# Prefix sums, slot placing and scatters of a routed graph network: each moved one tile later

## The reference

```python
def _sage_conv(x, edge_index, W_l, W_r, b):
    src, dst = (edge_index[0], edge_index[1])
    agg_sum = segment_sum(x[src], dst, num_segments=x.shape[0])
    agg = agg_sum / maximum(deg, 1.0)[:, None]
    return agg @ W_l + x @ W_r + b
h = relu(_sage_conv(layernorm(x), edge_index, W1_l, W1_r, b1))
x = x + _sage_conv(h, edge_index, W2_l, W2_r, b2)
tokens = layernorm(x)
probs = softmax(tokens @ router_w.T)
rw, re = top_k(probs, 2);  rw = rw / maximum(rw.sum(-1), 1e-12)
combine = zeros((N, 8)).at[arange(N)[:, None], re].set(rw)
out = tokens
for e in range(8):
    y = gelu(tokens @ w1[e] + b1[e]) @ w2[e] + b2[e]
    out = out + combine[:, e:e + 1] * y
return x + out
```

## Time and profile before

| what | us |
|---|---|
| median of 3 timed runs (617.13 to 617.48) | 617.24 |
| the profiled execution | 618.39 |
| span of its records | 616.7 |
| PE busy (90% of the span) | 553.9 |
| DVE busy (60%) | 367.0 |
| POOL busy (29%) | 181.9 |
| third stage, first row of the second aggregation to the first rows loaded for the experts | 293 to 478 |

### The profile page before, as it was taken

The page is one execution under the profiler, slowest core; times in us unless marked ns, Lnnn a source line. Parts: engine busy times, 40 slices in busy tenths (PEclk is TensorE's granted clock), DMA queues, the critical chain, the costliest instruction groups (busy, mean ns, idle before and its releaser), DMA issues.

```text
span 616.7 us, 11244 instructions
## 1 busy us (share of the span) xinstructions
PE 553.9 (90%) x3021; PEld 332.5 (54%) x3022; DVE 367.0 (60%) x1222; ACT 222.8 (36%) x422; POOL 181.9 (29%) x181
## 2 busy tenths in 40 slices
PE   5999989999999999999899999989960799998990
PEld 3544545555555555554354544545430688887880
DVE  5987656766676677662456676765767244443440
ACT  5666835434434444441001000000000355555550
POOL 3740000000000000000211434424355086668884
PEclk9999999999999999999999999999985699999995
DMA  8421211101111110113721347643226367677772
GB/s 267 124 73 60 69 36 52 52 27 52 52 43 36 52 51 28 51 53 56 246 86 53 129 144 242 193 152 129 88 84 230 89 118 129 117 123 115 128 113 30
DMA packets 64343, 61.24 MB, mean 99 GB/s; under 512 B 11281, under 2 KB 62334, under 8 KB 64302
## 3 DMA queue, kind: packets, MB, share of 16 engines
q1 hardware_dynamic: 47422, 44.84, 24.1%
q0 software_dynamic: 11200, 14.40, 12.7%
q10 hardware_dynamic: 5680, 1.49, 1.1%
HBM read 32.34 MB, written 29.30 MB: 100 GB/s over the span
## 4 chain that ended last, share of the span: by engine, by line
PE 61%; DVE 11%; issue 11%; POOL 7%; DMA 6%; ACT 1%; POOLq 1%; DVEq 0%; SPq 0%; ACTq 0%
PE bank L1262 21%; PE counts_ps L635 7%; PE counts_ps L1404 6%; PE bank L1252 6%; PE bank L1177 6%; PE bank L1415 6%; PE counts_ps L1262 4%; POOL xs_dram L570 4%; DMA out<-adj 2%; POOL stat L563 2%; PE counts_ps L1395 2%; POOL out L608 2%; DMA y<-y_dram 1%; PE bank L1167 1%; PE bank L1245 1%
## 5 line engine op out<-in xcount | busy, mean ns | idle before, releaser
L1262 PE MATMUL bank<-y,adj 128*128 128x512 f16 x625 | 154.7, 379 | 0.4 <-ACT zt L1470 0.4
L1262 PE MATMUL counts_ps<-y,adj 128*128 128x512 f16 x625 | 144.5, 379 | 1.9 <-DMA y<-y_dram 1.9
L642 ACT ACTIVATE adj<-counts_ps 128x1000 f32 (+1 forms) x80 | 80.2, 1004 | 61.2 <-PE counts_ps L635 61.2
L608 POOL DMA_INDIRECT out<-adj x56 | 87.0, 1554 | 47.7 <-ACT adj L1603 21.1
L1262 PEld LDWEIGHTS counts_ps<-y,adj 128*128 128x128 f16 x625 | 60.5, 101 | 64.8 <-DMA y<-y_dram 3.9
L1262 PEld LDWEIGHTS bank<-y,adj 128*128 128x128 f16 x625 | 57.8, 97 | 59.5 <-issue 13.7
L546 POOL IOTA onehots<- 128x8 int32 x1 | 0.1, 143 | 231.9 <-PE counts_ps L635 231.9
L1404 PE MATMUL counts_ps<-adj 128*128 128x256 f32 x240 | 58.6, 389 | 2.3 <-ACT adj L1588 2.3
L1567 ACT ACTIVATE rows<-bank 128x256 f32<-128x256 f32 x25 | 9.6, 382 | 128.7 <-PE bank L1336 128.7
L635 PEld LDWEIGHTS counts_ps<-onehots 125*128 125x128 f16 x640 | 41.0, 98 | 27.2 <-issue 10.8
L621 DVE TENSOR_TENSOR onehots<-iota,lo_t 125x1024 f16<-125x1024 f16 x80 | 54.7, 683 | 0.2
(11 more groups left out here) (234 smaller groups left out, 641.0 us busy)
## 6 DMA issues: line engine op xcount, KB each, us to landing
adj<-xs_dram SPq DMA_DIRECT2D x31, 264.0 KB
rows<-z_dram SPq DMA_DIRECT2D x49, 128.0 KB
z_dram<-zt SPq DMA_DIRECT2D x36, 128.0 KB, 1.7
adj<-in_L_ffn_w SPq DMA_DIRECT2D x16, 256.0 KB, 3.2
rows<-in_x SPq DMA_DIRECT2D x24, 128.0 KB
out<-yo SPq DMA_DIRECT2D x24, 128.0 KB
y_dram<-yo SPq DMA_DIRECT2D x23, 128.0 KB, 1.7
y<-y_dram SPq DMA_DIRECT2D x4, 640.0 KB, 6.6
```

The lines of the kernel that those rows point to most:

```text
L608: g.indirect_dma_start(out, bass.IndirectOffsetOnAxis(ap=ids[u][:, h:h + 1], axis=0), ye[u][:, h, :], None, bounds_check=N - 1, oob_is_err ...
L642: nc.scalar.activation(adj[:, :, bass.ds(at, GW * WD)].rearrange("p b (h d) -> p b h d", d=WD), counts_ps[:, 2 * (group % 2):2 * (group % ...
L1262: last = te.matmul(to, adj[:, b, t * P:(t + 1) * P], y[:, b, :], start=(b == 0), stop=(b == NT - 1))
```

## The change

The prefix sums of batches 0 to 4 move from the last block of tiles 5, 9, 13, 17, 21 to block 7 of tiles 6, 10, 14, 18, 22. `place` of these batches moves from the end of the second tile to the third tile, between `x2_and_var` and `norm_and_sum`. A tile is scattered six tiles later and no longer five; after the root of tile 23 two tiles, 17 and 18, are scattered, so that the end is as it was. And the wait for the landing of the scatter before, with its count, is kept only as long as a later tile uses the buffer again, which is up to tile 17.

```diff
-                if t > 0:
+                if 0 < t <= NT - KEPT:
                     pool.wait_ge(scattered[(t - 1) % 2], ((t - 1) // 2 + 1) * (16 * TOPK))
                     pool.sem_inc(S["tok_free"], 1)
...
                 if t == NT - 1:
                     scatter(*to_scatter[t - BATCH - 1])
                 root(t)
-                if BATCH + 1 <= t < NT - 1:
+                if BATCH + 2 <= t < NT - 1:
+                    scatter(*to_scatter[t - BATCH - 2])
+                if t == NT - 2:
                     scatter(*to_scatter[t - BATCH - 1])
...
             for t in range(NT):
                 x2_and_var(t)
+                j = t // BATCH
+                if t % BATCH == 2 and 0 < j < NB - 1:
+                    place(j - 1)
                 if t == NT - 1:
                     place(NB - 2)
                 norm_and_sum(t)
-                j = t // BATCH
                 if t % BATCH == 0 and 0 < j < NB - 1:
                     choose(j - 1)
-                if t % BATCH == 1 and 0 < j < NB - 1:
-                    place(j - 1)
+                if t % BATCH == 2 and 0 < j < NB - 1:
                     if j == MID_BATCH:
...
-                if t % BATCH == 1 and t // BATCH > 0 and t < FIRST_OF[NB - 1]:
-                    between[NT - 1] = [lambda: prefix(t // BATCH - 1)]
+                if t % BATCH == 2 and t // BATCH > 0 and t < FIRST_OF[NB - 1]:
+                    between[7] = [lambda: prefix(t // BATCH - 1)]
```

## The result

The changed kernel takes **611.59 us** (median of 4 runs, 611.18 to 612.18); the kernel before took 617.36 us beside it (4 runs, 617.13 to 618.30). The ratio is 0.990, with an interval from 0.989 to 0.992: 5.8 us are gone, and by the interval between 5.1 and 7.0. Predicted were 6.6 us and 610.6 us. The 6.6 us lie inside that interval too. The profiled execution took 611.19 us, its span is 609.5 us.

What follows compares the result with a forecast made beforehand. PE was taken to set the pace, losing time waiting for DVE's masks. Gains of 6.3 us from its stops and 0.3 from dropped waits made 6.6 us, from 617.24 to 610.6 us; forecast range 609.6 to 612.5, 8-in-10 range 609.4 to 613.0.

Steps and rivals of the forecast that it cites:

- PE sets the pace: Third stage, 293 to 478 us: PE loses time only waiting for DVE's masks; moving the prefix sums gains 6.3 us (5.7 to 6.5).
- a stop costs its record and 0.16 us more: PE's five stops at the prefix sums: each costs its recorded wait plus 0.16 us, 6.5 us together.
- The prefix sums inside the stream: PE's three small matmuls at block 7: taken as 0.04 us more than 0.09 for each batch.
- first rival: DVE's 16.57 us of 25 is the true pace and PE stops elsewhere: no change, 617.2 us; chance 0.06.
- The new place: Block 7 of the next tile, as in tile 10: the masks are there 0.9 us before PE asks.
- Tile 16's row: Input row that landed late and lengthened tile 17's wait to 1.87 us: counted 0, bound 0.5 us.
- `place`: DVE's 1.33 us step, moved into its idle time before normalization: cost 0, tightest transpose keeps 1.0 us to spare.
- Scatters a tile later: POOL's scatters, with six transfers instead of four between the roots of tiles 23 and 24: cost 0, bound 0.5 us.
- It fits by 0.04 us: POOL between the roots of tiles 23 and 24: two more transfers take 2.53 us of 2.57 idle.
- second rival: Part of the gain: masks later than block 7, or last root slips one transfer, 1.3 us; 613 us, chance 0.13.
- The dropped waits: POOL at the stage's end: last scatter 0.8 us sooner, gain 0.3 us at SP's first load, bounds 0 and 0.8.
- third rival: POOL's root and DVE's normalization form a ring without slack; `place` adds 0.57 us five times: 620.1 us, chance 0.04.

Runs made afterwards that it cites:

- block2: Changed kernel with the prefix sums ahead of block 2 instead of block 7 of the same tile; 614.43 us, ratio 0.994 to the kernel before.
- x_split: Changed kernel with the last tile's input row, 53 rows, loaded as 48 and 5; 611.25 us, ratio 0.990 to the kernel before.
- prefix_back: Changed kernel with the prefix sums alone put back to the last block of tiles 5, 9, 13, 17, 21; 616.68 us, ratio 0.999 to before.
- prefix_alone: Kernel before with only the prefix sums moved to block 7 of the next tile; 612.73 us, ratio 0.992 to the kernel before.
- late_wait_again: Second run of the changed kernel with the wait behind tile 17's transfers put behind tile 19's, on tile 18's landing; 613.02 us, ratio 0.992.
- waits_back: Changed kernel with the wait for the scatter before put back after every scatter; 611.80 us, ratio 0.992 to the kernel before.
- scatter_early: Changed kernel with a tile scattered five tiles later, as before the change; 627.85 us, ratio 1.017 to the kernel before.

## Why the prediction was right, and where it was not

**PE sets the pace: right.** 6.42 us of the stage went with PE's stops, predicted were 6.3 (5.7 to 6.5). That a stop costs its record and 0.16 us more held: a tile of 7.19 us became one of 6.05, 1.14 us for a recorded 0.96, and `block2` shows 0.16 to 0.18 us from the other side. The prefix sums inside the stream cost 6.05 - 5.97 = 0.08 us; I had taken 0.13.

**The first rival, no change: wrong.** DVE's work stayed the same (16.79 us of 25 where it was 16.57) and the stage got 6.4 us shorter. The row of PE's own waits had decided against it, and the measurement agrees with that row. The rule of the Trainium skill ("Perfetto Trace Analysis", section "Identifying the Most-Contended Engine") did not back this rival as the prediction says: it names two measures for TensorE, weight loads and useful work, and the prediction took only the first (12.47 of 25 us, below DVE's 16.57). By the second, an estimate from that page's BF16 peak of 78.6 TFLOP/s and some 100 matmuls of 128 x 128 x 512 in the 25 us, TensorE does 85% of what it could, more than DVE's 66%, and the rule points to TensorE.

**The new place: right**, 0.88 us to spare by the changed kernel's rows and 0.82 by `block2`, predicted 0.9.

**Tile 16's row: too small a bound.** I counted 0 and at most 0.5 us. Tile 18 takes 0.08, 0.22 and 0.97 us more than 6.05 in the three profiles of the changed kernel, and 0.75 in `x_split`. The moves of `place` and the scatters seem to help, as argued for `place` (a stop of 1.07 for 1.87 us in `prefix_back`, 0 to 1.0 us beyond 6.05 for 1.66 in `prefix_alone`, each of the two in one profile), but they do not close the case.

**`place`: right at cost 0.** The normalization behind it has no idle time, and the tightest transpose has 0.96 us to spare, predicted 1.0. No transpose waits.

**Scatters a tile later: the step that failed.** "It fits by 0.04 us" counted six transfers by their issue, 1.26 us each, and left out the wait that stands between them: behind tile 17's transfers POOL waits for tile 16's to land, and that took 1.5 us longer than the usual gap. The root of tile 24 slipped by 1.5 us (1.2 in two more profiles), the last slots by 1.27 (1.03). The bound of 0.5 us was less than half of it; the second rival had the place and nearly the size (one transfer, 1.3 us), for another reason. The count of the six transfers itself was right: without the wait, in `late_wait_again`, the root comes 0.1 us after the variance (452.48 and 452.38 us). In the profile of the changed kernel this term is what the sum lacks. It is not shown to separate 610.6 from the 611.6 measured: with the root repaired the time stayed, since the table then came last.

**The dropped waits: the rows have the predicted size, a gain in time is not shown.** The last scatter is issued 0.82 us sooner after the last slots and SP's load 0.33 us, predicted 0.8 and 0.3; the load 0.4 and 0.5 us sooner in two more profiles. But in these the slots are late as well, so the 0.33 us is not the work of the waits alone. `waits_back` shows no difference in time and no later load, and where the root is on time DVE stops, and nothing of the gain is left.

**The third rival, slower: wrong.** No transpose waits, and `place` between variance and normalization costs nothing. In `scatter_early` the same two engines do hold each other up, but by another link, the scatter's wait for the slots; at 627.85 us it costs more than the 620 that the rival gave its own.

**The sum.** 6.42 + 0.33 - 1.27 = 5.5 us by the trace, 5.8 by the timed runs (5.1 to 7.0), 6.6 predicted. In the trace the two terms of cost that I set to nothing make the difference: the scatters with 1.27 us, and tile 16's row with 0.08 us here and up to 1.0 elsewhere. One of them had a row against it, the 2.75 us of the earlier trace rows. That the total still fell into the range of the forecast is in part luck: the scatters went beyond their bound, and the other terms came out well.

## What to carry to other kernels

If the engine that sets the pace stops for a result, move the consumer down its list until the result is there with time to spare, and count a stop as its recorded idle time plus what the record of the instruction ahead of it is too long. Then follow every in-order queue that the delayed result passes: a scatter that waits for it must not stand ahead of something that the pace needs. When more issues are put into a gap, add up the waits between them too; a fit by 0.04 us leaves room for none. And a repaired delay is worth only what the next thing to come last allows: here the root came 1.2 us sooner, and the experts' table took its place.

## What the runs showed that I had not expected

- A load of 53 rows of 1 KB ran at 0.07 of the sixteen engines and 25 GB/s; one of 48 and one of 5 rows were over sooner. The Trainium skill says why ("DMA: Bandwidth & Descriptors", section "Why a DMA increments its semaphore by 16 and not by 1"): the number of engines is the largest up to 16 that divides the outer dimension of both sides of the transfer, which is 1 for 53 rows. The trace agrees, with 0.07 of the engines. Beside this load POOL waited 0.6 to 1.5 us longer for the landing of scatters from another queue, by four profiles against one without it.
- DVE stood still, in seven profiles, for up to 3.34 us between two instructions on tiles that it writes itself, always while the DMA engines were at about 1.0 and above 300 GB/s. The page of the profile lists instruction packets among the DMA queues, but not when they ran; whether DVE waited for its own code or for something else stays open.
- A running stream of matmuls took in the three small matmuls of the prefix sums for 0.08 us (6.05 us a tile against 5.97).
